# Four chained cross-attentions on one core: a fourth set of buffers and a new written-out order that puts alike TensorE steps side by side

## The chip, the core and the metric

The kernel runs on one core of a Trainium2 chip, in one launch. A core has five engines with instruction streams of their own: TensorE (PE in the profile, its weight loads PEld), VectorE (DVE), ScalarE (ACT), GpSimd (POOL) and SyncE (SP, which here only issues transfers). They meet through semaphores. All data are 32-bit floats. The metric is the device time of one launch in microseconds (us); lower is better. Matrix results go to PSUM, which the kernel treats as eight banks of 128 partitions by 512 floats.

## What is computed

128 batches of 64 query tokens (128 channels) attend to 64 context tokens (256 channels), four layers in a row. Layer 0 has 16 heads of 64 and a bias on a few key columns; layers 1 to 3 normalise x, have 16 query heads of 8 and 4 key/value heads. Cut to what matters:

```python
# layer 0
q = x @ Wq; k = ctx @ Wk; v = ctx @ Wv                 # 16 heads of 64
logits = einsum('bhqd,bhkd->bhqk', q, k) * 64 ** -0.5 + col_bias
out = einsum('bhqk,bhkd->bhqd', softmax(logits), v)
x = reshape(out) @ Wo + bo + x
# layers 1, 2, 3
xn = x * rsqrt(mean(x * x) + eps) * norm_w
q = xn @ wq; k = ctx @ wk; v = ctx @ wv                # 16 query heads of 8, 4 of k and v
scores = einsum('btgrd,bsgd->bgrts', q, k) / sqrt(8)
x = x + einsum('bgrts,bsgd->btgrd', softmax(scores), v) @ wo
```

## The kernel before

Four batches make a group (`G = 4`, 256 tokens); there are `NG = 32` groups. A group passes through named steps, written (kind, group, layer, unit). In the code they are branches of one loop per engine:

- TensorE, full 128x128 passes: `k` (L942, four steps), `v` (L954, six), `k3` (L961, keys of layers 1 to 3), `q0` (L969, four), `wo0` (L1027, the output projection of layer 0), and for each later layer `q` (L1032), `x2` (L1038, x transposed by full 128x128 passes, two into one bank, for the sum of squares) and `wo` (L1063).
- TensorE, with the array split into tiles: `s` of layer 0 (L980, 64x64, two steps), `s` of layers 1 to 3 (L991, 32x64, one step, four banks), `t` (L1009, the probabilities transposed, 64x128), `pv0` (L1019, 64x64, two steps) and `pv` (L1055, 128x32).
- VectorE: `add` (L1213), `max` (L1220, L1226), `sub` (L1230), `sum` (L1235), `rcp` (L1238), `wo0`, `wo` (L1257, residual added), `ssq`. GpSimd: `sub` of layer 0 (L888), `nrm` (L892, probabilities times 1/sum), `ms`. ScalarE: `exp` (L1136), `et` (L1141, the transposed probabilities copied from PSUM back to `E`), and the copies of `k`, `v`, `q0`, `pv0`, `x2`, `q`, `pv` out of PSUM. A group and layer have four units u of 128x512 probabilities each.

So the chain of one layer is q, s, max, sub, exp, sum, rcp, nrm, t, et, pv, wo, and then the next layer's q and x2. TensorE is kept at work meanwhile by the other groups in flight. A group's buffers (`xT`, `QT`, `E`, `st`, `nt`, `inv`) are chosen by `g % NS`, with `NS = 3`.

The order on each engine is written out: tables of numbers (`PE_TIME` and others) give every step a slot, group g is shifted by `g * PERIOD`, other tables (`PE_ENDS` and others) replace the numbers for the first and last groups, and `timed` sorts. The slots serve as sort keys; the engines wait on semaphores and on nothing else. In groups 30 and 31 (`SPLIT`) the later layers go in halves, and there the normalisation follows `pv` (L1049, L1248).

The PSUM banks are dealt out at build time. The loop walks the TensorE order; `free[i]` holds when the present contents of bank i are due to be emptied, by the table slots (`DUE`), and a step takes the bank or banks with the smallest `free`. Steps `s` of layers 1 to 3 take two neighbouring pairs:

```python
at = min(([i, i + 1, j, j + 1] for i in range(5) for j in range(i + 2, 7)),
         key=lambda four: max(free[i] for i in four))
```

At run time the step first waits until the step that emptied its bank has really ended (`emptied`), wherever its slot was.

## Time and profile before

| | |
|---|---|
| median of three runs | 1381.56 us (1379.52 to 1381.87) |
| span of the profiled execution | 1376.3 us |
| PE busy | 1362.7 us, 99% of the span |
| DVE, ACT, POOL busy | 1064.6, 1003.3, 734.9 us |
| PE in the chain that ended last | 95% |
| granted TensorE clock | full speed in every slice |

The median is 5.3 us above the profiled span; that is what lies around the span in a timed run. In a timeline row the first number is the start in us from the start of the span, the second the length, then engine, line, operation, what is written and read, the shape, and how many were merged into the row. A 32-bit matmul leaves two records; a transpose leaves one. The length of a PE row runs over the start of the next, since the array is pipelined, so the time that a block takes of PE is read from its start to the start of the next row. "[0.99 <-issue]" says that PE sat idle for that long before the row, and that no semaphore ended it.

### The profile page before, as it was taken

Reading aid. Unit: us, or ns where it says so; the run is one execution under the profiler, and the core shown is the slowest. Engines: PE = TensorE matmul, PEld = TensorE weight load, DVE = VectorE, ACT = ScalarE, POOL = GpSimd, SP = SyncE. Lnnn points to the kernel's source line nnn. Section 1 sums busy time; section 2 is a strip of 40 time slices with the busy share of each in tenths; the row PEclk is TensorE's granted clock in tenths of the full one; section 3 lists DMA queues with packets and bytes.
Section 4 is the critical chain, followed back from the end, with each engine's and each line's share of the span. In section 5 each row is a group of like instructions: output and inputs, shape, how many; then the busy total and the mean of one; then the engine's idle time right before and its main releaser. Section 6 shows DMA issues by size and latency. Waiting matters only on the chain.

```text
span 1376.3 us, 59054 instructions
## 1 busy us (share of the span) xinstructions
PE 1362.7 (99%) x25494; PEld 1055.6 (77%) x25494; DVE 1064.6 (77%) x2258; ACT 1003.3 (73%) x2207; POOL 734.9 (53%) x851
## 2 busy tenths in 40 slices
PE   9999999999999999999999999999999999999997
PEld 7777777777777777777787777777777777777875
DVE  4487777987778977778777788777798777778776
ACT  4667777767778677777677786777776777767886
POOL 5355456654456545466554565544665445655553
PEclk9999999999999999999999999999999999999999
DMA  5010010000000010100001001001011010010000
GB/s 151 18 30 22 15 34 16 26 27 23 26 23 22 27 27 23 28 18 26 26 24 26 23 22 27 27 24 28 17 27 27 23 27 25 19 36 22 7 23 14
DMA packets 46003, 37.02 MB, mean 27 GB/s; under 512 B 17072, under 2 KB 41520, under 8 KB 45744
## 3 DMA queue, kind: packets, MB, share of 16 engines
q1 hardware_dynamic: 44576, 32.89, 8.8%
q8 instruction: 201, 3.29, 1.0%
q14 instruction: 58, 0.48, 0.1%
q10 hardware_dynamic: 1168, 0.36, 0.1%
HBM read 16.42 MB, written 4.19 MB: 15 GB/s over the span
## 4 chain that ended last, share of the span: by engine, by line
PE 95%; ACT 2%; DVE 2%; issue 0%; POOL 0%; DMA 0%; SPq 0%; POOLq 0%
PE psum L954 18%; PE psum L942 16%; PE psum L1009 10%; PE psum L1027 8%; PE psum L969 8%; PE psum L991 7%; PE psum L1055 7%; PE psum L1019 5%; PE psum L980 5%; PE psum L1063 4%; PE psum L1032 3%; PE psum L961 2%; PE psum L1038 2%; ACT E L1141 1%; ACT E L1136 1%; DVE st L1226 1%
## 5 line engine op out<-in xcount | busy, mean ns | idle before, releaser
L892 POOL TENSOR_TENSOR E<-E,st 128x512 f32<-128x512 f32 x488 | 497.3, 1044 | 168.1 <-DVE st L1238 159.4
L1136 ACT ACTIVATE E<-E,inv 128x512 f32<-128x512 f32 x384 | 273.4, 722 | 135.8 <-DVE E L1230 134.3
L1226 DVE TENSOR_REDUCE st<-psum 128x8 f32<-128x512 f32 x372 | 240.4, 673 | 145.5 <-PE psum L991 145.1
L1235 DVE TENSOR_REDUCE st<-E 128x8 f32<-128x512 f32 x488 | 321.2, 665 | 35.3 <-ACT E L1129 28.2
L1141 ACT COPY E<-psum 128x512 f32<-128x512 f32 x512 | 275.1, 609 | 33.7 <-PE psum L1009 33.5
L954 PE MATMUL psum<-wv,cT 128*128 128x374 f32 (+1 forms) x768 | 273.3, 486 | 0.3 <-issue 0.3
L1230 DVE TENSOR_TENSOR E<-psum,st 128x512 f32<-128x512 f32 x372 | 248.3, 677 | 0.3
L904 POOL TENSOR_TENSOR nt<-nt,powers 128x2 f32<-128x2 f32 (+1 forms) x102 | 19.9, 196 | 420.0 <-DVE nt L1265 400.2
L942 PE MATMUL psum<-cT,wk 128*128 128x256 f32 x1024 | 240.5, 383 | 0.2 <-DMA cT<-in_ctx_t 0.2
L942 PEld LDWEIGHTS psum<-cT,wk 128*128 128x128 f32 x1024 | 191.5, 190 | 34.8 <-issue 1.5
L954 PEld LDWEIGHTS psum<-wv,cT 128*128 128x128 f32 x768 | 138.2, 189 | 73.5 <-ACT V L1097 8.5
L888 POOL TENSOR_TENSOR E<-E,st 128x512 f32<-128x512 f32 x140 | 142.6, 1044 | 35.8 <-DVE st L1220 13.1
L1009 PE MATMUL psum<-ident,E 64*128 64x64 f32 x4096 | 156.6, 226 | 3.5 <-issue 1.4
L1009 PEld LDWEIGHTS psum<-ident,E 64*128 64x128 f32 x4096 | 138.3, 139 | 20.0 <-issue 8.0
L969 PE MATMUL psum<-xq,wq 128*128 128x256 f32 x512 | 129.0, 385 | 0.0
L1027 PE MATMUL psum<-QT,wo 128*128 128x256 f32 (+1 forms) x544 | 119.1, 372 | 0.5 <-ACT QT L1163 0.5
L1055 PEld LDWEIGHTS psum<-E,VB 128*32 128x32 f32 x6144 | 90.9, 110 | 37.1 <-issue 14.7
L1097 ACT COPY V<-psum 128x374 f32<-128x374 f32 (+1 forms) x192 | 87.3, 456 | 42.9 <-PE psum L954 42.1
L1121 ACT ACTIVATE QT<-psum 128x512 f32<-128x512 f32 x128 | 75.9, 599 | 56.5 <-PE psum L969 48.2
L969 PEld LDWEIGHTS psum<-xq,wq 128*128 128x128 f32 x512 | 94.8, 190 | 23.1 <-issue 10.8
L991 PE MATMUL psum<-KB,QT 32*64 32x256 f32 x3072 | 109.2, 388 | 1.6 <-ACT QT L1160 1.0
L1027 PEld LDWEIGHTS psum<-QT,wo 128*128 128x128 f32 x544 | 96.2, 190 | 14.8 <-ACT QT L1163 0.6
(68 smaller groups left out, 1632.2 us busy)
## 6 DMA issues: line engine op xcount, KB each, us to landing
KB<-K SPq DMA_DIRECT2D x1536, 8.0 KB
cT<-in_ctx_t SPq DMA_DIRECT2D x32, 256.0 KB, 2.8
xq<-in_x_t SPq DMA_DIRECT2D x32, 128.0 KB, 2.1
out<-xT SPq DMA_DIRECT2D x30, 128.0 KB, 1.8
wk<-in_L_xattn_Wk SPq DMA_DIRECT2D x3, 256.0 KB, 5.8
wv<-in_L_xattn_Wv SPq DMA_DIRECT2D x2, 374.0 KB, 8.6
wq<-in_L_xattn_Wq SPq DMA_DIRECT2D x1, 512.0 KB, 7.7
wo<-in_L_xattn_Wo SPq DMA_DIRECT2D x1, 512.0 KB, 4.4
```

Of the source, the lines that this page charges most:

```text
L892: e.tensor_tensor(E3, E3, wide(stat[s][u][:, 16:24]), ALU.mult).then_inc(g_nrm.sem, 1)
L942: m = e.matmul(bank[:, T * jj:T * jj + T], wk0[:, k, 128 * j:128 * j + 128], cTg[:, k, :], start=(k == 0), stop=(k == 1))
L954: m = e.matmul(bank[:, 0:hi - lo], cTg[:, k, 128 * p:128 * p + 128], wv[:, k, lo:hi], start=(k == 0), stop=(k == 1))
L969: m = e.matmul(bank[:, T * jj:T * jj + T], wq0[:, 128 * j:128 * j + 128], xq[g % NX][:, :], start=True, stop=True)
L991: m = e.matmul(psum[64 * b2:64 * b2 + 64, at[r], 256 * p:256 * p + 256], QT[s][lo:lo + 32, 0, 64 * b:64 * b + 64], KB[l - 1][g % 2][lo:lo ...
L1009: m = e.transpose(psum[:, at[2 * n + i], c:c + 64], E[s][2 * p + r][rows, 128 * k:128 * k + 128], ident[rows, rows])
L1027: m = e.matmul(bank[:, tokens], wo0[:, j, :], QT[s][:, j, tokens], start=(j == 0), stop=(j == 7))
L1136: e.activation(E[s][u][:, :], E[s][u][:, :], ACT.Exp, scale=inv[s][:, u // 2:u // 2 + 1]).then_inc(a_exp.sem, 1)
L1141: e.copy(E[s][u][:, :], psum[:, i, :]).then_inc(a_et.sem, 1)
L1226: e.tensor_reduce(stat[s][u][:, 0:8].rearrange("p (r h) -> p r h", r=2), scores_of[g, l, u], AX, ALU.max).then_inc(d_max.sem, 1)
L1230: e.tensor_tensor(pairs(E[s][u][:, :]), scores_of[g, l, u], stat[s][u][:, 0:8].rearrange("p (r h a) -> p r h a", r=2, a=1).to_broadcast([1 ...
L1235: e.tensor_reduce(stat[s][u][:, 8:16], heads(E[s][u][:, :]), AX, ALU.add).then_inc(d_sum.sem, 1)
```

## The change

Three things differ; what is computed stays.

1. `NS` is 4 where it was 3, so four groups have buffers at a time.
2. All tables are new, with `PERIOD` 40.556641 where it was 42.042923. The tables for single groups now cover groups 0 to 7 and 28 to 31, and replace a group's table as a whole. Step `t` of groups 0 to 29 becomes two steps, one for two units each, with two banks instead of four and a wait of its own.
3. `DUE` is the slot plus a length by kind (`TAKES`), where it was the slot alone. The banks are dealt out anew from it. In the new tables for groups 28 to 31 a long row of steps has one and the same time: 16 of TensorE's steps stand at 1229.03 and 22 at 1270.13.

```diff
-NS = 3
+NS = 4
-PERIOD = 42.042923
+PERIOD = 40.556641
...
-    "t": {0: (-348.90236,), 1: (-317.45557,), 2: (-285.56016,), 3: (-253.49293,)},
+    "t": {0: (66.71164, 66.21564), 1: (98.14828, 97.59927), 2: (135.04492, 133.99991), 3: (176.09756, 175.10556)},
...
-        for kind, layers in {**table, **{k: {**table.get(k, {}), **v} for k, v in at_ends.get(g, {}).items()}}.items():
+        for kind, layers in at_ends.get(g, table).items():
...
-DUE = {tuple(st): at for at, *st in ACT_TIMED + DVE_TIMED}
+TAKES = {"k": 0.59, "v": 0.48, "k3": 0.36, "q0": 0.6, "pv0": 1.09, "x2": 0.39, "q": 0.37, "pv": 0.36, "se": 0.6, "et": 0.61,
+         "exp": 0.72, "add": 0.68, "max": 0.68, "sub": 0.68, "sum": 0.67, "rcp": 0.19, "wo0": 0.47, "ssq": 0.41, "lr": 0.33,
+         "lm": 0.29, "wo": 0.42}
+DUE = {(kind, g, l, u): at + (1.1 if kind == "v" and u % 3 == 2 else TAKES[kind])
+       for at, kind, g, l, u in ACT_TIMED + DVE_TIMED}
...
             if kind == "t":
-                return [[("et", g, l, 2 * p + i)] for p in halves(g, u) for i in range(2)]
+                return [[("et", g, l, 2 * u + i)] for i in range(2)]
...
-        p_t = signal("p_t", [("t", g, l, p) for _, g, l, u in of(PE_ORDER, "t") for p in halves(g, u)])
+        p_t = signal("p_t", of(PE_ORDER, "t"))
...
-                if kind != "t":
-                    emptied(w, [ev for evs in before[st] for ev in evs])
+                emptied(w, [ev for evs in before[st] for ev in evs])
...
-                    for n, p in enumerate(halves(g, u)):
-                        emptied(w, before[st][2 * n] + before[st][2 * n + 1])
-                        if late(g, l):
-                            w.wait_ge(a_exp, ("exp", g, l, 2 * p), ("exp", g, l, 2 * p + 1))
...
+                    if late(g, l):
+                        w.wait_ge(a_exp, ("exp", g, l, 2 * u), ("exp", g, l, 2 * u + 1))
...
-                    i = bank_of["t", g, l, part(g, u // 2)][u % 2 if g in SPLIT else u]
+                    i = bank_of["t", g, l, u // 2][u % 2]
```

Counted over the whole of TensorE's order, the new one goes from a full pass to a tiled step 159 times, where the old one did 235 times. Unbroken blocks of one tiled kind: `t` 104 for 131, `pv` 38 for 97, `pv0` 35 for 59, `s` of layers 1 to 3 98 for 102, `s` of layer 0 34 for 34. The number of matmuls is the same, 14891.

**Place 1, TensorE in the middle of the program.** L1055 or L1378 is `pv`, L1009 or L1332 is `t`, L980 or L1305 `s` of layer 0, KB and QT belong to `s`, wos to `wo`. Before, from one `pv` on:

```order
L1055 MATMUL psum<-E_0,VB 32x64 x8
L1055 MATMUL psum<-E_1,VB 32x64 x8
L1055 MATMUL psum<-E_2,VB 32x64 x8
L1055 MATMUL psum<-E_3,VB 32x64 x8
L1009 MATMUL psum<-ident,E_0 128x64 x8
L1009 MATMUL psum<-ident,E_1 128x64 x8
L1009 MATMUL psum<-ident,E_2 128x64 x8
L1009 MATMUL psum<-ident,E_3 128x64 x8
L1063 MATMUL psum<-QT,wos 128x256
L954 MATMUL psum<-wv,cT 128x372 x2
L1038 MATMUL psum<-ident,xT 128x128 x2
L1032 MATMUL psum<-xT,wqs 128x256
```

After, at the like place, from the second step of `s` of layer 0 on (four further rows of the third `pv` follow):

```order
L1305 MATMUL psum<-KT,QT 64x64 x64
L1332 MATMUL psum<-ident,E_2 128x64 x8
L1332 MATMUL psum<-ident,E_3 128x64 x8
L1332 MATMUL psum<-ident,E_0 128x64 x8
L1332 MATMUL psum<-ident,E_1 128x64 x8
L1378 MATMUL psum<-E_0,VB 32x64 x8
L1378 MATMUL psum<-E_1,VB 32x64 x8
L1378 MATMUL psum<-E_2,VB 32x64 x8
L1378 MATMUL psum<-E_3,VB 32x64 x8
L1378 MATMUL psum<-E_0,VB 32x64 x8
L1378 MATMUL psum<-E_1,VB 32x64 x8
L1378 MATMUL psum<-E_2,VB 32x64 x8
```

The `t`, `s` and `pv` steps of three groups now stand in one tiled stretch, where single ones stood between full passes. It begins with eight rows of `t` ahead of the ones shown.

**Place 2, TensorE at `s` of layer 3 in the middle of the program,** with the semaphores that a row waits for; a_et counts the copies `et`. Before (the `s` of group 16):

```order
L1063 MATMUL psum<-QT1,wos 128x256 [waits a_ev]
L954 MATMUL psum<-wv,cT0 128x374 x2
L1032 MATMUL psum<-xT1,wqs 128x256 [waits d_ev,d_add]
L1038 MATMUL psum<-ident,xT1 128x128 [waits a_et]
L1038 MATMUL psum<-ident,xT1 128x128
L954 MATMUL psum<-wv,cT0 128x374 x2
L991 MATMUL psum<-KB2_0,QT1 64x256 [waits l_kb2_0,a_et,a_ev]
L991 MATMUL psum<-KB2_0,QT1 64x256 x15
L954 MATMUL psum<-wv,cT0 128x372 [waits a_ev]
```

After (the `s` of group 16; E2 and `t` are those of layer 0 of group 18):

```order
L1332 MATMUL psum<-ident,E2_2 128x64 [waits g_nrm,a_ev]
L1332 MATMUL psum<-ident,E2_2 128x64 x7
L1332 MATMUL psum<-ident,E2_3 128x64 x8
L1332 MATMUL psum<-ident,E2_0 128x64 [waits g_nrm,a_ev]
L1332 MATMUL psum<-ident,E2_0 128x64 x7
L1332 MATMUL psum<-ident,E2_1 128x64 x8
L1316 MATMUL psum<-KB2_0,QT0 64x256 [waits d_ev,l_kb2_0,a_et,a_ev]
L1316 MATMUL psum<-KB2_0,QT0 64x256 x15
L1267 MATMUL psum<-cT1,wk0 128x256 x4
```

The `s` now stands directly behind a `t`, and one of its four banks is the one that this `t` filled first. That is so in 12 groups: 3, 8, 9, 11, 13, 14, 16, 18, 19, 21, 23 and 24.

**Place 3, TensorE at `s` of layer 1 of group 28,** with waits; d_sub counts VectorE's subtractions. Before:

```order
L969 MATMUL psum<-xq2,wq0 128x256 [waits a_ev]
L969 MATMUL psum<-xq2,wq0 128x256
L1063 MATMUL psum<-QT2,wos 128x256
L991 MATMUL psum<-KB0_0,QT1 64x256 [waits l_kb0_0,d_sub,a_ev]
L991 MATMUL psum<-KB0_0,QT1 64x256 x15
L954 MATMUL psum<-wv,cT2 128x374 [waits d_ev]
L954 MATMUL psum<-wv,cT2 128x374
L969 MATMUL psum<-xq2,wq0 128x256 [waits a_ev]
L969 MATMUL psum<-xq2,wq0 128x256
```

After:

```order
L1286 MATMUL psum<-cT0,wks 96x256 [waits d_sub]
L1286 MATMUL psum<-cT0,wks 96x256
L1316 MATMUL psum<-KB0_0,QT0 64x256 [waits a_ev,l_kb0_0,d_sub]
L1316 MATMUL psum<-KB0_0,QT0 64x256 x15
L1361 MATMUL psum<-ident,xT0 128x128 x2
L1294 MATMUL psum<-xq2,wq0 128x256 [waits l_xq2,d_sub]
L1294 MATMUL psum<-xq2,wq0 128x256 x3
L1294 MATMUL psum<-xq2,wq0 128x256 [waits a_ev]
L1294 MATMUL psum<-xq2,wq0 128x256
```

Behind the `s`, only an `x2` stands before a `q0` (L1294) that waits for d_sub: it has been dealt a bank that this very `s` filled, and waits for the third of its four subtractions. The same pair stands at `s` of layer 1 of group 29, with `q0` directly behind it. Behind `s` of layer 3 of group 27 stands a `v` of that kind, again for the third of four. Between groups 27 and 30 banks pass from step to step in other places too. With nothing between the two users of a bank stand: nine steps that wait for one copy of ScalarE (`pv0` of group 27 and of 28, `v` and `q` around them, `q0` of 29 and of 30, three `pv`), four that wait for one `wo` of VectorE, and, by `et`, twice each: the second `t` of layer 2 (with one `t` between), `s` of layer 0 behind four `t`, the second `t` of layer 1 into the banks of the first, for both of its copies, and the `pv` behind that. In the order before no step takes over a bank that the step directly ahead of it filled. Early in the new order there are two more: an `s` of layer 0 in group 9 (behind its own first step) and the `s` of layer 2 of group 8 (behind a `pv0`).

## Rows read from the trace of the kernel before

**Rows 1.** The page: busy us of each engine, share of the span, instructions.
```profile
PE 1362.7 (99%) x25494; PEld 1055.6 (77%) x25494; DVE 1064.6 (77%) x2258; ACT 1003.3 (73%) x2207; POOL 734.9 (53%) x851
```

**Rows 2.** Busy time by window: the last 44 us before the end.
```profile
1333.00:1377.00 44.00, 35.23 (x1016) 25.92 (x1004) 30.75 (x58) 29.79 (x72) 14.97 (x25) 1.00 0.06 17
```

**Rows 3.** Timeline of PE: the same step of two neighbouring groups (start, length, what).
```profile
560.15 3.62 PE L942 MATMUL psum<-cT,wk 128*128 128x256 f32 x16
...
601.99 1.24 PE L942 MATMUL psum<-cT,wk 128*128 128x256 f32 x5
```

**Rows 4.** Timeline of PE, 605 to 623: blocks and what follows each.
```profile
605.54 1.10 PE L1055 MATMUL psum<-E,VB 128*32 128x64 f32 x64
606.57 1.21 PE L1009 MATMUL psum<-ident,E 64*128 64x64 f32 x32
607.71 0.70 PE L1063 MATMUL psum<-QT,wos 128*128 128x256 f32 x2
608.25 1.41 PE L954 MATMUL psum<-wv,cT 128*128 128x372 f32 x4
...
609.71 0.60 PE L1032 MATMUL psum<-xT,wqs 128*128 128x256 f32 x2
610.24 1.16 PE L1019 MATMUL psum<-E,V 64*64 64x64 f32 x64
611.33 1.21 PE L1009 MATMUL psum<-ident,E 64*128 64x64 f32 x32
...
622.42 0.59 PE L1063 MATMUL psum<-QT,wos 128*128 128x256 f32 x2
622.85 0.38 PE L1038 MATMUL psum<-ident,xT 128*128 128x128 f32 x2
```

**Rows 5.** Timeline of PE: blocks of other lengths, each with the row behind it.
```profile
34.23 2.10 PE L1019 MATMUL psum<-E,V 64*64 64x64 f32 x128
36.25 1.99 PE L942 MATMUL psum<-cT,wk 128*128 128x256 f32 x8
...
1305.37 1.71 PE L1009 MATMUL psum<-ident,E 64*128 64x64 f32 x48
1307.01 1.52 PE L954 MATMUL psum<-wv,cT 128*128 128x374 f32 x4
...
1359.33 0.63 PE L1055 MATMUL psum<-E,VB 128*32 128x64 f32 x32
1359.89 1.07 PE L1063 MATMUL psum<-QT,wos 128*128 128x128 f32 x4
```

**Rows 6.** Waits of PE; the page's instruction queue; PE at 632; that queue in 631.50 to 631.75.
```profile
PE psum L1009 <- issue: 1.4, 2, 1.0
PE psum L1019 <- issue: 0.8, 3, 0.3
...
q8 instruction: 201, 3.29, 1.0%
...
632.05 0.90 PE L1009 MATMUL psum<-ident,E 64*128 64x64 f32 x22
633.94 0.53 PE L1009 MATMUL psum<-ident,E 64*128 64x64 f32 x10 [0.99 <-issue]
...
q8 instruction: 1, 0.02, 23.9%
```

**Rows 7.** Timeline of all engines: a transpose and the copy that empties its first bank.
```profile
589.77 1.21 PE L1009 MATMUL psum<-ident,E 64*128 64x64 f32 x32
...
590.53 0.59 ACT L1141 COPY E<-psum 128x512 f32<-128x512 f32 x1 [0.76 <-PE psum L1009]
```

**Rows 8.** Timeline: scores of a group, PE's next block, VectorE's third subtraction of them.
```profile
573.64 1.12 PE L991 MATMUL psum<-KB,QT 32*64 32x256 f32 x32
574.69 1.10 PE L1055 MATMUL psum<-E,VB 128*32 128x64 f32 x64
...
579.06 0.68 DVE L1230 TENSOR_TENSOR E<-psum,st 128x512 f32<-128x512 f32 x1
```

More of the change, by code:

```diff
@@ new lines @@
+    "sum": {0: (62.37469, 63.30765, 60.96066, 61.55667),
+            1: (90.35269, 92.57068, 93.16669, 93.76270),
+            2: (121.89328, 121.18826, 123.47629, 124.66830),
+            3: (164.62894, 163.43692, 161.14890, 165.92996)},
+    "rcp": {0: (63.08371, 65.05463, 62.97070, 62.26569),
+            1: (91.06171, 94.58072, 94.35870, 94.47171),
+            2: (126.56531, 131.50534, 127.59631, 130.80032),
+            3: (172.28400, 165.82095, 162.34091, 169.45795)},
+    "wo0": {0: (81.93265,)},
@@ L106 @@
-    "lt": {0: (-85.21396,)},
-    "st": {0: (-22.10277,)},
+    "cT": {0: (107.54190,)},
+    "kr": {1: (4.32867,), 2: (55.93527,), 3: (68.51465,)},
+    "lt": {0: (148.57855,)},
+    "st": {0: (241.79120,)},
 }
@@ new lines @@
+        "v": {0: (54.61811, 72.22778, 60.19144, 49.69811, 50.95478, 69.14044)},
+        "k3": {0: (53.75478,)},
+        "q0": {0: (48.83478, 58.46478, 64.43144, 59.32811)},
+        "s": {0: (68.09644, 67.11645), 1: (92.42812,), 2: (118.09644,), 3: (147.26279,)},
+        "t": {0: (79.52578, 77.81944),
+              1: (104.53478, 103.98578),
+              2: (138.26678, 137.71777),
+              3: (175.26511, 174.27312)},
+        "pv0": {0: (82.32411, 80.16978)},
+        "wo0": {0: (85.24678,)},
@@ new lines @@
+    4: {
+        "k": {0: (0.47821, 19.61655, 22.74222, 7.55588)},
+        "v": {0: (32.03989, 69.21321, 46.43622, 9.28255, -0.88245, 61.58421)},
+        "k3": {0: (2.63655,)},
+        "q0": {0: (41.94855, 43.46155, 50.67622, 45.46889)},
+        "s": {0: (54.74655, 53.76656), 1: (84.64522,), 2: (114.01822,), 3: (149.94354,)},
+        "t": {0: (65.64755, 65.09856), 1: (97.42822, 96.87921), 2: (134.45889, 133.41388), 3: (176.04355, 175.05154)},
+        "pv0": {0: (72.08655, 71.10056)},
+        "wo0": {0: (75.63321,)},
+        "x2": {1: (83.46889,), 2: (105.65622,), 3: (146.56488,)},
+        "q": {1: (83.03722,), 2: (111.46356,), 3: (145.91522,)},
+        "pv": {1: (99.84122,), 2: (138.70987,), 3: (180.72455,)},
+        "wo": {1: (104.36121,), 2: (144.62021,), 3: (186.57220,)},
+    },
@@ new lines @@
+        "et": {0: (77.19067, 77.19116, 77.19043, 77.19092),
+               1: (103.68823, 103.68799, 103.68774, 103.68750),
+               2: (165.42786, 164.94983, 161.93787, 163.03784),
+               3: (195.09155, 194.61353, 191.31348, 193.65747)},
+        "pv0": {0: (77.19238, 77.19214)},
+        "x2": {1: (94.87109,), 2: (133.86682,), 3: (173.55249,)},
+        "q": {1: (94.87085,), 2: (140.05188,), 3: (172.87354,)},
+        "pv": {1: (128.69482,), 2: (168.38989,), 3: (197.48145,)},
@@ new lines @@
+        "kr": {1: (58.15911,), 2: (80.25911,), 3: (91.30911,)},
+        "lt": {0: (158.56912,)},
+        "st": {0: (227.26912,)},
+    },
+    1: {
+        "cT": {0: (117.53247,)},
+        "kr": {1: (28.65247,), 2: (61.80247,), 3: (84.38247,)},
+        "lt": {0: (152.12247,)},
+        "st": {0: (187.67247,)},
+    },
+    2: {
+        "cT": {0: (111.08583,)},
+        "kr": {1: (32.29583,), 2: (54.87582,), 3: (77.93582,)},
+        "lt": {0: (145.67583,)},
+        "st": {0: (187.05981,)},
+    },
@@ new lines @@
+    3: {
+        "cT": {0: (104.63919,)},
+        "kr": {1: (25.36920,), 2: (48.42918,), 3: (71.48920,)},
+        "lt": {0: (106.07919,)},
+        "st": {0: (187.19385,)},
+    },
+    4: {
+        "cT": {0: (102.52621,)},
+        "kr": {1: (18.92255,), 2: (41.98254,), 3: (69.37622,)},
+        "lt": {0: (103.00623,)},
+        "st": {0: (187.72589,)},
+    },
+    5: {
+        "cT": {0: (101.13257,)},
+        "kr": {1: (12.47591,), 2: (39.86958,), 3: (67.98257,)},
+        "lt": {0: (101.61258,)},
+        "st": {0: (188.78925,)},
+    },
```

1128 lines of the change are left out of this document (690 added, 438 removed), and 88 rows, old and new, of tables (DVE_ENDS, PE_ENDS).

## The prediction, made before the changed kernel ran

> **What bounds the kernel now.** I read the page first. TensorE is busy for 1362.7 us, 99% of the span; the others have slack [rows 1]. TensorE idles mainly in the last 44 us, where 35.23 are busy and 8.8 are lost to hand-offs [rows 2]. In the middle there is next to none: the same step of two neighbouring groups starts at 560.15 and 601.99, 41.84 us apart [rows 3]. So the time is the length of TensorE's own list of steps, plus what it waits. A faster or slower neighbour changes nothing until TensorE waits for it.
>
> Next I read how long a block takes of TensorE, from its start to the start of the next row. A `wo` between full passes takes 0.43 us (622.42 to 622.85). A `wo` behind a `t` takes 0.54 (607.71 to 608.25), and a `q` of the same size ahead of a `pv0` takes 0.53 (609.71 to 610.24) [rows 4]. Going into tiled work and coming back costs 0.10 each. The tiled blocks have a fixed part too: `t` takes 1.64 us for 48 records [rows 5] and 1.14 for 32 [rows 4], so 0.50 for 16 and 0.14 for the block; `pv` 1.03 for 64 [rows 4] and 0.56 for 32 [rows 5], so 0.09 for the block; `pv0` 2.02 for 128 [rows 5] and 1.09 for 64 [rows 4], so 0.16. With such lengths laid end to end the old order gives 41.86 us for a group, against the 41.84 that I read. I trust them.
>
> **What the change removes.** The same matmuls run. Visits to tiled work fall from 235 to 159: 76 x 0.20 = 15.2 us. Blocks fall by 27 for `t` (x 0.14 = 3.8), by 59 for `pv` (x 0.09 = 5.3) and by 24 for `pv0` (x 0.16 = 3.8). The four fewer of `s` are left out. In sum 28 us go, all of them on the path, since TensorE is the path. The new order laid end to end gives 40.8 us for a group. The unknown is whether two `pv` of different groups join as cheaply as two halves of one; if not at all, 5.3 us less is saved, so 23 to 30.
>
> **What it adds: waits for banks.** A step can't start until its bank has been copied out. What that costs when nothing stands between the two users is read off a `t`: the block starts at 589.77, its first bank is full 0.64 us later (0.14 + 0.50), the copy starts at 590.53 and takes 0.59 [rows 7]. That is 0.12 to get there and 0.59 for the copy; I take as long again for the way back, 0.83 in all. No row shows such a pair, so its bounds are nothing, if the copy has some other way to be early, and 1.3, when the second copy is the one waited for.
>
> Middle: the `s` of layer 3 stands directly behind a `t` and needs its first bank in 12 groups (place 2). 12 x 0.83 = 10 us; bounds 0 and 16.
>
> Late groups (place 3). Three steps wait for the third subtraction of an `s` just ahead. In the trace an `s` starts at 573.64 and gives way at 574.69; VectorE's third subtraction of it starts at 579.06 and takes 0.68, so it ends 5.05 us after the `s` [rows 8]. VectorE has four maxima, three subtractions and a little more to do before that point, in the new order as well. With the `x2` in between (0.2) that is 4.8 and 5.0; the third, where one row of sums falls out, 4.5. Sum 14.3. Behind the waiting `q0` or `v` the whole of TensorE's queue stands still. Nine steps wait for one short copy: between the way alone (0.24) and a `t`'s 0.83, I take 0.6, as these copies are of half a bank: 5.4. Four wait for a `wo` of VectorE, also half a bank: 0.65 each, 2.6. Those by `et`, twice each: 0.83 less the 0.50 of the `t` between is 0.33, then 0.83, then both copies 1.33, then 0.83, together 6.6. The late groups lose 14.3 + 5.4 + 2.6 + 6.6 = 29 us. Bounds: 14 if only the three long ones bite, 35 if each short one costs a `t`'s.
>
> **What it adds: instruction supply.** TensorE idles in the middle almost only with "issue" named, 1.4 us in two places at `t` and 0.8 in three at `pv0`; the longest, 0.99, lies inside the `t` block that starts at 632.05 and resumes at 633.94. A transfer of the instruction queue begins 2.2 to 2.4 us before that end, in the window from 631.50. There are 201 such transfers of 3.29 MB, 16.4 KB each [rows 6]. TensorE has 25494 records, each with a weight load [rows 1], so one transfer brings about 254 instructions. Two steps `s` of layer 0 are 128 records or 256 instructions in 2.03 us: there TensorE runs out. Cut into lots of 254 along the block lengths, the old order has 6 to 8 lots that pass in under 2.4 us, the new one 36 to 38, for now `pv0` stands in pairs and `pv` in threes (384 instructions in under 3 us). Measured against the usual length of their kind, the blocks before are 3.8 us too long in total, 0.5 for each such lot. At 0.4 to 0.5 the new order would lose 14 to 20. I take 16, so 12 more than before; bounds 2 (a lot costs only what it falls short of 2.2 us) and 18.
>
> The Trainium skill ("Runtime: NRT & Kernel Launch", Instruction fetch mechanics) says that instructions stream in blocks of 16 KiB and that crossing into the next one is mostly hidden. The block size agrees with 16.4 KB; on the hiding, the 0.99 us speaks against it in dense stretches. By that rule this term would be nothing; it is the second rival.
>
> **What else.** The end: `t`, `pv` and `wo` of three and four groups stand together there, so the last results come out together and the chains have less beside them. Before, 8.8 us are lost in 44 [rows 2]. I take 6 more; bounds 0 and 12. Early groups have two bank pairs and a start with more to fill: 2, bounds 0 and 8. The fourth set of buffers costs nothing itself: it takes waits on older groups away, and TensorE had none of those.
>
> **The sum**, against the profiled execution: 1376.3 - 28 + 10 + 29 + 12 + 6 + 2 = 1407.3 us of span. The median of the runs lies 5.3 above the span: 1412.5 us. All low ends together give 1381.6 - 30 + 0 + 14 + 2 + 0 + 0 = 1368, all high ones 1381.6 - 23 + 16 + 35 + 18 + 12 + 8 = 1448.
>
> **The rivals.**
>
> *The banks come free in time.* The waits written into the order would then be met at once, because TensorE reaches those steps late or the copies run ahead. What is left is 1381.6 - 28 + 12 + 6 + 2 = 1373.5, faster than before. It decides at 8 us: if all bank waits together cost less, the change wins. For it speaks that in the old trace nearly every such wait is met early. Against it speaks that a copy can't start before the step that fills the bank ends, and here the next user stands directly behind.
>
> *Instructions come in time*, by the page's rule above. Then this term is -3.8 instead of +12: 1396.5. For it: only a few of the dense places before show idle time.
>
> *The chains are too tight in the middle.* In the old order 17.3 us of TensorE's work lie between `s` of layer 0 and its `t`, in the new one 10.2, with twelve passes of VectorE over 128x512 (at 0.6 to 0.68 us [rows 8]) in the chain. If `t` is late by 0.5 to 1 us in each group, 14 to 28 us come on top: about 1430. Against it: for layers 1 to 3 the distance grows or stays. Here also falls the case that joined blocks save nothing beyond the visits, 13 us, 1425.5.
>
> **How the numbers follow.** The forecast, 1412.5 with its own range of 1402 to 1424, has a chance of 0.60; banks in time 0.07; instructions in time 0.18; tight chains 0.12; something that none of these names 0.03. The range of 8 in 10 takes in the second rival and most of the third: 1392 to 1431. What a measurement can tell from no change is 0.2%, or 2.8 us. Only the first rival ends below 1378.8. Faster 0.07, same 0.03, slower 0.90.
>
> **What would show it.** In the profile after: distances of 40.8 us plus one or two waits between like steps of middle groups; in 12 of them 0.7 to 0.9 us of idle time ahead of the `s` of layer 3 with `et` named; three idle times of 4 to 5 us of TensorE with a subtraction of VectorE named, between 1180 and 1280, at `q0`, `v` and `q0`; some 15 us of idle time in tiled blocks put to "issue". A `q0` there without such a wait breaks the largest term. If the time is below 1380, it is the bank waits that I have wrong; if above 1431, the chains in the middle.

## The result: 8.4% slower, in the predicted direction and nearly four times the predicted amount

| | before | after |
|---|---|---|
| median | 1381.7 us | 1498.3 us |
| ratio, 95% interval | | 1.0843 [1.0826, 1.0861] |
| span of the profiled execution | 1376.3 us | 1494.2 us |
| PE busy | 1362.7 us, 99% | 1368.3 us, 92% |

I had forecast 1412.5, with 1392 to 1431 as the range. One of the four executions after took 1631.0 us at a granted clock of 0.84; the ratio leaves it out, and without it the median is 1497.4.

One number of the text ahead has to be set right here. Nearly every execution on record takes some 1.8 us more than its own span (the profiled one after: 1496.05 with a span of 1494.2). So of the 5.3 us between the median before and the profiled span only some 1.8 lie around the span; the rest is the difference between one execution and another. The forecast stays as it is, since its 31 us come on top of a median.

The page of the changed kernel: busy time and record counts, the granted clock in 40 slices, the instruction queue, and the chain of work that ended last (95% of it was TensorE before).

```profile
PE 1368.3 (92%) x25494; PEld 1074.8 (72%) x25494; DVE 1069.2 (72%) x2258; ACT 1010.3 (68%) x2207; POOL 734.6 (49%) x851
...
PEclk9999999999999999999999999999999999999998
...
q8 instruction: 201, 3.29, 0.9%
...
PE 62%; DVE 20%; ACT 12%; issue 6%; POOL 0%
```

The work is the same as in [rows 1]: same records, nearly the same busy time. What grew is the time in which TensorE stands still. Its waits (line waited at, who ended the wait: us in total, times, longest) name two kinds:

```profile
PE psum L1378 <- issue: 46.6, 37, 2.2
PE psum L1316 <- issue: 11.3, 17, 0.8
PE psum L1294 <- DVE E L1553: 9.3, 2, 4.7
PE psum L1332 <- issue: 5.1, 8, 1.0
...
PE psum L1279 <- DVE E L1553: 4.9, 2, 4.6
PE psum L1305 <- issue: 4.8, 10, 1.0
```

L1378 is `pv`, L1316 `s` of layers 1 to 3, L1332 `t`, L1305 `s` of layer 0, L1294 `q0`, L1279 `v`. Where [rows 6] had 1.4 and 0.8 us put to "issue", there are now 70.7. Twelve of the 17 waits at L1316 stand at the first record of a step; all the others put to "issue", 64 with 62.0 us, stand inside a block of one kind.

**Where the time went.** I took TensorE's order laid end to end, with the block lengths of the prediction, and cut it at the `wo0` of group 3 and of group 27. Before (L1027) and after (L1350):

```profile
156.08 3.72 PE L1027 MATMUL psum<-QT,wo 128*128 128x256 f32 x16
...
1164.27 3.72 PE L1027 MATMUL psum<-QT,wo 128*128 128x256 f32 x16
...
166.25 3.72 PE L1350 MATMUL psum<-QT,wo 128*128 128x256 f32 x16
...
1235.19 3.72 PE L1350 MATMUL psum<-QT,wo 128*128 128x256 f32 x16
```

| stretch | before: read, laid | after: read, laid | laid changes by | loss over laid changes by |
|---|---|---|---|---|
| to `wo0` of 3 | 156.1, 149.3 | 166.3, 153.7 | +4.4 | +5.8 |
| to `wo0` of 27 | 1008.2, 1003.7 | 1068.9, 979.6 | -24.1 | +84.8 |
| to the end | 212.0, 194.9 | 259.0, 186.1 | -8.8 | +55.8 |
| sum | 1376.3, 1347.9 | 1494.2, 1319.4 | -28.5 | +146.4 |

So the saving is there, 28.5 us, and 146.4 are lost on top: +117.9 of span. The laid lengths are an estimate from rows, good to some us.

**The middle.** TensorE's timeline in one group of it (start, length, line, what, records, idle time before):

```profile
716.93 2.20 PE L1332 MATMUL psum<-ident,E 64*128 64x64 f32 x64
719.23 2.14 PE L1305 MATMUL psum<-KT,QT 64*64 64x64 f32 x128
721.30 0.52 PE L1332 MATMUL psum<-ident,E 64*128 64x64 f32 x9
722.70 0.90 PE L1332 MATMUL psum<-ident,E 64*128 64x64 f32 x23 [0.89 <-issue]
723.53 1.66 PE L1378 MATMUL psum<-E,VB 128*32 128x64 f32 x104
727.19 1.44 PE L1378 MATMUL psum<-E,VB 128*32 128x64 f32 x88 [2.00 <-issue]
...
735.83 1.12 PE L1316 MATMUL psum<-KB,QT 32*64 32x256 f32 x32 [0.72 <-issue]
```

The stops at 722.70 and 727.19 lie in the middle of a step, where no semaphore is waited for. Between the two resumptions lie 23 + 104 = 127 records, 254 instructions with the weight loads: one lot, as the prediction calls what one transfer of the instruction queue brings. Transfers of that queue start at 720.25, 724.27 and 728.42; in the window from 724.25 to 724.50 it is

```profile
q8 instruction: 1, 0.02, 35.7%
```

TensorE resumes at 722.70 and 727.19, 2.5 and 2.9 us after the start of the transfer ahead. So it is throughout: all 59 stops inside a block up to 1235 us end 2.2 to 3.0 us after the start of a transfer. In 29 places a stop is followed by another 126 to 128 records behind, 3.3 to 4.5 us later, 3.8 on average. The second of such a pair is 1.35 us long on average, the other 35 stops 0.65: lots in a row are what costs.

Over the 25 groups from 100 to 1250 us the blocks of three `pv` are 52.9 us longer than the same block laid out (0.8 to 3.6 each), the two `s` of layer 0 and the `t` behind them 19.5.

The `s` of layer 3 behind a `t` waits 0.72 or 0.73 us in 12 groups, 8.7 in sum. They are just the 12 groups of place 2. In seven others between groups 5 and 22 the `s` stands behind a `t` too, but has been dealt other banks, and waits for nothing. So this wait is one for the bank, though the trace names "issue".

**The late groups.** The three long waits, where they were expected:

```profile
1293.85 4.24 PE L1294 MATMUL psum<-xq,wq 128*128 128x256 f32 x12 [4.60 <-DVE E L1553]
...
1331.23 2.86 PE L1279 MATMUL psum<-wv,cT 128*128 128x374 f32 x4 [4.57 <-DVE E L1553]
...
1354.04 3.78 PE L1294 MATMUL psum<-xq,wq 128*128 128x256 f32 x8 [4.66 <-DVE E L1553]
```

and busy time by window (last columns: granted clock, DMA share, GB/s):

```profile
1290.00:1376.00 86.00, 63.78 (x1166) 48.91 (x1166) 47.80 (x104) 46.36 (x99) 38.61 (x43) 0.92 0.05 15
...
1406.00:1494.00 88.00, 66.96 (x1874) 51.78 (x1871) 57.32 (x110) 56.70 (x129) 38.93 (x56) 0.92 0.04 11
```

22.2 and 21.0 us idle; the last 88 us before had 8.2. And the clock is not at full speed here, as it was in every slice before. From the `wo0` of group 27 on, TensorE is idle 48.2 us, where it was 8.8: 39.4 of the 55.8. Of the rest some 10 go to the clock, an estimate that the last part works out; some 6 stay open.

### The profile page after: what moved, and what is told of

The parts are those of the page before. It is cut to its first block, busy times and chain, and to the rows that moved or that the text cites. A ratio compares the mean times of both kernels' runs of the same rounds, so it can differ in the third digit from the quotient of the medians.

```text
span 1494.2 us, 58934 instructions
## 1 busy us (share of the span) xinstructions
PE 1368.3 (92%) x25494; PEld 1074.8 (72%) x25494; DVE 1069.2 (72%) x2258; ACT 1010.3 (68%) x2207; POOL 734.6 (49%) x851
## 4 chain that ended last, share of the span: by engine, by line
PE 62%; DVE 20%; ACT 12%; issue 6%; POOL 0%
PE psum L1267 11%; PE psum L1279 10%; PE psum L1332 7%; PE psum L1378 7%; DVE st L1549 6%; DVE st L1558 6%; PE psum L1316 6%; DVE E L1553 5%; PE psum L1305 4%; ACT E L1459 4%; PE psum L1342 4%; PE psum L1294 3%; PE psum L1350 3%; PE psum L1386 3%; ACT E L1464 2%
## 5 line engine op out<-in xcount | busy, mean ns | idle before, releaser
L1558 DVE TENSOR_REDUCE st<-E 128x8 f32<-128x512 f32 x488 | 310.5, 671 | 90.5 <-ACT E L1452 55.7
L1549 DVE TENSOR_REDUCE st<-psum 128x8 f32<-128x512 f32 x372 | 240.3, 682 | 117.9 <-PE psum L1316 117.8
L1459 ACT ACTIVATE E<-E,inv 128x512 f32<-128x512 f32 x384 | 260.7, 719 | 88.0 <-DVE E L1553 83.9
L1464 ACT COPY E<-psum 128x512 f32<-128x512 f32 x512 | 262.3, 617 | 37.9 <-PE psum L1332 36.8
L1279 PE MATMUL psum<-wv,cT 128*128 128x374 f32 (+1 forms) x768 | 278.1, 486 | 6.6 <-DVE E L1553 4.9
L1267 PE MATMUL psum<-cT,wk 128*128 128x256 f32 x1024 | 249.5, 387 | 1.2 <-issue 1.0
L1553 DVE TENSOR_TENSOR E<-psum,st 128x512 f32<-128x512 f32 x372 | 241.1, 678 | 1.5
L1279 PEld LDWEIGHTS psum<-wv,cT 128*128 128x128 f32 x768 | 143.5, 192 | 79.1 <-issue 10.3
L1332 PE MATMUL psum<-ident,E 64*128 64x64 f32 x4096 | 154.6, 227 | 13.0 <-issue 5.1
L1332 PEld LDWEIGHTS psum<-ident,E 64*128 64x128 f32 x4096 | 138.3, 139 | 38.3 <-issue 23.6
L1378 PE MATMUL psum<-E,VB 128*32 128x64 f32 x6144 | 106.4, 222 | 50.9 <-issue 46.6
L1536 DVE TENSOR_TENSOR E<-psum,bias 128x512 f32<-128x512 f32 x128 | 82.2, 683 | 88.7 <-PE psum L1305 88.7
L1420 ACT COPY V<-psum 128x276 f32<-128x276 f32 (+1 forms) x192 | 84.4, 440 | 85.0 <-PE psum L1279 85.0
L1378 PEld LDWEIGHTS psum<-E,VB 128*32 128x32 f32 x6144 | 93.4, 111 | 61.2 <-issue 54.3
L1294 PE MATMUL psum<-xq,wq 128*128 128x256 f32 x512 | 127.0, 389 | 10.7 <-DVE E L1553 9.3
L1316 PE MATMUL psum<-KB,QT 32*64 32x256 f32 x3072 | 114.0, 392 | 15.7 <-issue 11.3
L1294 PEld LDWEIGHTS psum<-xq,wq 128*128 128x128 f32 x512 | 96.2, 194 | 31.7 <-DVE E L1553 10.0
L1350 PE MATMUL psum<-QT,wo 128*128 128x256 f32 (+1 forms) x544 | 117.1, 369 | 0.6 <-ACT QT L1469 0.4
```

Source lines behind the costliest of these rows:

```text
L1267: m = e.matmul(bank[:, T * jj:T * jj + T], wk0[:, k, 128 * j:128 * j + 128], cTg[:, k, :], start=(k == 0), stop=(k == 1))
L1279: m = e.matmul(bank[:, 0:hi - lo], cTg[:, k, 128 * p:128 * p + 128], wv[:, k, lo:hi], start=(k == 0), stop=(k == 1))
L1294: m = e.matmul(bank[:, T * jj:T * jj + T], wq0[:, 128 * j:128 * j + 128], xq[g % NX][:, :], start=True, stop=True)
L1316: m = e.matmul(psum[64 * b2:64 * b2 + 64, at[r], 256 * p:256 * p + 256], QT[s][lo:lo + 32, 0, 64 * b:64 * b + 64], KB[l - 1][g % 2][lo:lo ...
L1332: m = e.transpose(psum[:, at[i], c:c + 64], E[s][2 * u + r][rows, 128 * k:128 * k + 128], ident[rows, rows])
L1378: m = e.matmul(bank[32 * r:32 * r + 32, 64 * b:64 * b + 64], VBg[:, b, c:c + 32], E[s][b][:, n:n + 64], start=(gp == 0), stop=(gp == 1))
```

## The experiments

My theory after the result: (1) in the middle, instructions don't come fast enough, and lots that follow each other cost far more than the single ones of the old trace; (2) in the late groups, the banks. The rivals: steps of different groups don't join on the array, the chains of the groups are too tight, the fourth set of buffers costs. All ratios are to the kernel before, run on the same chip at the same time (1380.1 to 1381.8 us).

**The supply by itself.** The kernel before, with this ahead of its first step:

```diff
+            for n in (64, 96, 112, 128):
+                for i in range(320):
+                    r = i % 4
+                    e.matmul(psum[32 * r:32 * r + 32, 7, 0:n], blank[:, 0:32], blank[:, 0:n], start=True, stop=True)
+                for _ in range(32):
+                    e.matmul(psum[:, 6, 0:128], blank, blank, start=True, stop=True)
```

> The kernel before with dense work ahead of everything else: four stretches of 320 tiled matmuls (128x32 tiles, four column groups in turn, blank data) of 64, 96, 112 and 128 columns, each followed by 32 full passes of 128 columns. They write to a bank that is overwritten later, so the output stays. A stretch is five lots of 254 instructions. By the pace of a pv (32 matmuls of 64 columns in 0.94 us) the stretches would take 9.4, 14.1, 16.5 and 18.8 us. Theory A (a lot can't be fetched before the one ahead of it has begun, and lots that follow each other take about 4.1 us each, as read from the changed kernel): 64 columns about 2.2 us of idle time per lot, 96 columns 1.3, 112 columns 0.8, 128 columns 0.4; put to issue. Theory B (my prediction's: a lot costs 0.4 to 0.5 us when it passes in under 2.4 us, otherwise nothing): 0.5 per lot at 64 columns, nothing at 96 and above. Theory C (nothing to do with instructions): no idle time at all. Whole time by A about 1460 us, by B about 1450, by C about 1447.

Measured 1482.96 us in one run. Timeline of PE, the stretches of 64, 96, 112 and 128 columns:

```profile
12.38 3.38 PE L925 MATMUL psum<-E 128*32 128x64 f32 x128 [4.37 <-issue]
17.75 2.77 PE L925 MATMUL psum<-E 128*32 128x64 f32 x128 [1.99 <-issue]
21.48 2.30 PE L925 MATMUL psum<-E 128*32 128x64 f32 x128 [0.96 <-issue]
...
33.36 5.81 PE L925 MATMUL psum<-E 128*32 128x96 f32 x271
39.80 2.84 PE L925 MATMUL psum<-E 128*32 128x96 f32 x128 [0.63 <-issue]
43.53 2.85 PE L925 MATMUL psum<-E 128*32 128x96 f32 x128 [0.88 <-issue]
47.53 2.55 PE L925 MATMUL psum<-E 128*32 128x96 f32 x113 [1.16 <-issue]
...
66.08 3.27 PE L925 MATMUL psum<-E 128*32 128x112 f32 x128 [0.46 <-issue]
69.81 3.27 PE L925 MATMUL psum<-E 128*32 128x112 f32 x128 [0.46 <-issue]
73.26 1.41 PE L925 MATMUL psum<-E 128*32 128x112 f32 x49 [0.18 <-issue]
...
81.94 17.67 PE L925 MATMUL psum<-E 128*32 128x128 f32 x640
```

From stop to stop there are always 128 records. The distance between two stops is 3.73 us in most cases, with 64, 96 and 112 columns alike (17.75 to 21.48, 39.80 to 43.53, 66.08 to 69.81). It is no fixed floor: the others are 5.37 (12.38 to 17.75), 4.00 (43.53 to 47.53) and 3.45 (69.81 to 73.26). The 5.37 falls into a time when the data come in (all queues together moved 311 GB/s from 13 to 18 us, 5 at most from 26 us on); whether that is the reason was not tested. With 128 columns a lot takes 17.6 / 5 = 3.5 by itself, and no stop is seen. The first lots of a stretch pass: 271 records of 96 columns run without a stop, two lot boundaries among them, though a lot takes 2.84 there; the third boundary costs 0.63, the next 0.88 and 1.16.

So the threshold in my prediction was wrong, and the price with it. A lot is short when it passes in under 3.5 to 4 us, not under 2.4, and once a few short ones have followed each other, each costs the difference. Theory A had the kind of it right, and the pace nearly (4.1); it had named 0.4 per lot at 128 columns, where there is none. B and C fall by the rows. The whole time decides nothing, as 1483 lies above all three (1460, 1450, 1447): they had left some 8 us for the full passes between the stretches, an estimate, and 64 records of these take 7.41, four times. The Trainium skill ("Runtime: NRT & Kernel Launch", Instruction fetch mechanics) calls the crossing from one block of instructions to the next mostly hidden. That agrees with the stretch of 128 columns and not with the other three.

**Does the stop follow the instructions?** The changed kernel with half a lot more at the start:

```diff
+            for i in range(32):
+                e.matmul(psum[32 * (i % 4):32 * (i % 4) + 32, 7, 0:64], blank[:, 0:32], blank[:, 0:64], start=True, stop=True)
```

> The changed kernel, with 32 tiled matmuls (64 records, about 128 instructions, half a lot) more at the very start, where TensorE waits for its first data anyway. Theory A (the idle time inside a block stands where a lot of about 254 instructions begins): in the block of three pv in which TensorE stands still behind record 104 of 192 (at 725.2 us of the changed kernel) it now stands still about 64 records earlier, behind record 40, and the one behind record 9 of 32 of the t ahead moves into s of layer 0. The whole time moves by less than 10 us either way. Rival (it stands where data or the array decide): it stays behind record 104.

Measured 1509.7 us in one run. The same group as above (L1307 is `s` of layer 0, L1334 `t`, L1380 `pv`):

```profile
723.49 1.42 PE L1307 MATMUL psum<-KT,QT 64*64 64x64 f32 x74
725.07 1.04 PE L1307 MATMUL psum<-KT,QT 64*64 64x64 f32 x54 [0.15 <-issue]
...
727.17 0.77 PE L1380 MATMUL psum<-E,VB 128*32 128x64 f32 x40
728.96 1.99 PE L1380 MATMUL psum<-E,VB 128*32 128x64 f32 x128 [1.02 <-issue]
732.29 0.54 PE L1380 MATMUL psum<-E,VB 128*32 128x64 f32 x24 [1.34 <-issue]
```

Behind record 40, as expected to the record; the one in `t` has moved into `s` (record 74, 9 - 64 + 128 = 73 expected), and a second boundary now falls into the same block of `pv` (40 + 128 + 24 = 192). The data and the array are as before. The stop belongs to the place in the stream of instructions. The whole time moved by 11 us, a little more than the 10 that I had allowed; 1 us of it is the added work itself (the `v` that starts at 18.00 starts at 19.03 here), for TensorE was not idle where it stands.

**Fewer instructions in the same order.**

```diff
...
-                        for gp in range(2):
+                        for gp in range(1 if g < NG - 4 else 2):
...
```

> The changed kernel, with the second half of the matmuls of every pv left out in groups 0 to 27 (the values of one of the two halves of heads are missing from the output). The order is unchanged, the three pv still stand together. 84 steps get 0.47 us shorter, 39 us. Theory A (instruction supply): the three together are then 192 instructions instead of 384, the 53 us of idle time in them vanish too: 1498 - 39 - 53 = about 1406, down to 1395 if the idle time at the t behind shrinks too. Rival (the join of different groups costs about 0.7 us whatever its length): 1459.

Measured 1430.8 (1.0366 [1.0350, 1.0382]): 67 us less, 28 more than the left out work. That lies between the two, 1406 and 1459; 25 us of what theory A has did not go. The waits at `pv`:

```profile
PE psum L1378 <- ACT E L1464: 12.0, 19, 0.7
PE psum L1378 <- issue: 10.0, 16, 1.1
```

The stops named issue went from 46.6 to 10.0, as theory A has it. But 12.0 us now go to the copies of `t` (L1464), where it was 2.3: the block ahead is shorter and covers them no more. The steps are joined as before, so a fixed cost of the join, the rival's 0.7 us, is not what the stops were.

**Passes between the pv.** In groups up to 29 a `k` or `v` from behind goes between two `pv` in a row:

```diff
...
+            for pv in run:
+                mixed += [pv] + behind[len(mixed) // 2:len(mixed) // 2 + 1]
...
```

> The changed kernel, with a k or v step of TensorE from behind put between pv steps that stand in a row (groups up to 29), and its copy on ScalarE moved with it; nothing else. The changed kernel is at 1498. Theory A (instruction supply): the 53 us by which the blocks of three pv are too long in the middle go nearly all; two more visits to tiled work per group (0.20 each) and two more blocks (0.09 each) cost 14 us in 25 groups: about 1460, and the idle time named issue inside pv falls from 47 us to under 5. Rival (the three-fold block is slow since the steps of different groups don't join: what is lost is lost per step): apart they would each still be too long, and the time stays at 1498 or above.

Measured 1469.9 (1.0651 [1.0634, 1.0669]): 28 us less than the change as it is. "Issue" at `pv` is 8.9 us where it was 46.6. Here L1404 is `pv`, L1342 `s` of layers 1 to 3:

```profile
PE psum L1342 <- issue: 12.2, 17, 1.2
PE psum L1404 <- issue: 8.9, 13, 1.1
```

The order laid end to end is 15.7 us longer, since every parting costs a visit to tiled work and a block. By the profiled spans (1494.2 and 1470.8) 39 us of loss went and 16 of the saving. I had expected 1460, with under 5 us of issue at `pv`; the parted blocks still hold an occasional stop. The rival, 1498 or above, falls.

**The banks.**

```diff
...
+        elif kind == "s":
...
+                    DUE[e, g, l, i] = now + LAG[e] + 0.68 * (i % 2 if l == 0 or g in SPLIT else i)
...
```

> The changed kernel, with the due times of the banks in the stretch of slots 1140 to 1290 taken from TensorE's list laid end to end (with 0.85 to 1.5 us for a copy and 4.0 and more for the subtractions, never earlier than the one ahead in its queue), instead of the slots of the copies. Orders are unchanged; only banks are dealt otherwise. Theory A (the waits in the late groups come from banks dealt by slots that all read 1229.03 and 1270.13): the waits of 4.60, 4.57 and 4.66 us and most short ones go, 21 us of the 29; the granted clock of 0.91 to 0.93 behind them goes to 1.00 and gives back about 5: 1498 - 26 = 1472. Rival (the waits stand for the chains of the late groups, which end when they end): the time stays within 5 us of 1498, idle time comes back with other names.

Measured 1477.2 (1.0711 [1.0684, 1.0738]), 21 us less, where I had expected 26. No order was touched. A window of this kernel, and a row of its timeline:

```profile
1290.00:1333.00 43.00, 40.74 (x760) 32.28 (x754) 32.08 (x69) 31.31 (x68) 22.57 (x26) 1.00 0.08 23
...
1339.61 1.85 PE L1330 MATMUL psum<-xq,wq 128*128 128x256 f32 x4 [3.51 <-DVE E L1589]
```

Two of the three long waits are gone, and so is the fall of the clock between 1290 and 1333 (0.93 in the changed kernel); one wait of 3.51 is left, and behind it four records of `q0` take 1.85 us, not 1.03.

**Both together.**

> The changed kernel with both edits that helped alone: passes between the pv steps (alone 1469.9, 28 us less) and due times of the late stretch from TensorE's list (alone 1477.2, 21 us less). If the two losses are separate things, as my theory has it (instruction supply in the middle, banks in the late groups), their gains add: 1498.3 - 28.4 - 21.1 = 1449. Rival (both are the same lack of slack seen twice): the gains overlap, and it stays above 1458.

Measured 1447.5 (1.0473 [1.0458, 1.0488]). By the medians the gains add within 2 us; by the ratios, each to the kernel before of its own time, the two alone give 45 us and both together 51, which is at the edge of the noise. They do not overlap, so instruction supply and late banks are two separate losses. With both edits the kernel is still 66 us slower than before: TensorE is idle for 77.6 us of the profiled 1453.8, 37.0 of them named issue, and the granted clock is 0.95 from 1235 us on. No run takes these apart.

**All passes spread.** With the new due times, four full passes per group go between tiled steps (two `pv` also change places where their copies come in the other order):

```diff
...
+MOVES = (("v", 1, 3, "s", 0, 0, 1), ("k", 1, 1, "t", -1, 1, 1), ("v", 0, 5, "pv", -1, 1, 0), ("v", 0, 1, "s", -2, 3, 0))
...
```

> The changed kernel with two edits. First, the due times of the banks in the late stretch as in the run before (1477). Second, in groups 5 to 28 four full passes go to new places of TensorE's order and their copies with them: a v between t and s of layer 0, a k between s of layer 0 and the t behind, a v between the first and the second pv, and a v between t and s of layer 3. Theory A (what is lost in the middle is instruction supply and the bank wait at s of layer 3): of 53 us at pv, 20 at s of layer 0 and the t behind, and 9 at s of layer 3, some 70 go, while four more visits to tiled work and the blocks that they cut cost 1.0 per group, 23 us: 1477 - 70 + 23 = 1430; idle time named issue falls from 68 to under 15 us. Rival (the chains of the groups are the limit, as in my third rival): TensorE waits for named engines instead, the time stays above 1455.

Measured 1526.9 (1.1059 [1.1041, 1.1077]): 97 us slower than expected, and 50 slower than with the due times alone. The waits (L1369 `s` of layers 1 to 3, L1385 `t`, L1439 `wo`):

```profile
PE psum L1369 <- DVE E L1606: 20.7, 19, 1.1
PE psum L1385 <- POOL E L1271: 17.1, 40, 1.3
...
PE psum L1439 <- ACT QT L1539: 7.4, 29, 0.7
```

The rival has it: named engines, and a time above 1455. Theory A is right in one part only: "issue" fell to 15.8 us in all. But now every group waits for named engines: `t` for the normalisation (it stands 1.25 us earlier), `s` of layer 2 for a bank of `s` of layer 3 (passes between them were taken away), `wo` for copies that stand behind a moved one. In this order the chains had no slack for such moves, so my third rival is real once passes are moved. I did not find an order that has both the joins and the slow lots; whether there is one stays open.

**The other term: buffers.**

> The kernel before, with a fourth set of buffers for the groups and nothing else. My prediction: costs and gives nothing, 1380 to 1383 us. Rival (some waits on the buffers of three groups before bind in the old order): up to 5 us faster. Another (the larger footprint costs): slower.

Measured 1381.25, 0.9998 [0.9989, 1.0007]. Nothing, as predicted.

**The clock.** Ahead of each of the three steps that wait long:

```diff
...
+                if st in KEEP:
+                    emptied(w, [ev for evs in before[KEEP[st]] for ev in evs])
+                    for _ in range(10):
+                        e.matmul(psum[:, bank_of[KEEP[st]][0], 0:T], ident[:, :], wk0[:, 0, 0:T], start=True, stop=True)
...
```

> The changed kernel, with ten full passes of 256 columns that nobody needs (4.3 us) ahead of each of the three steps that wait 4.6 us for a subtraction (q0 and v of group 29, q0 of group 30), into a bank that is free then. Theory A (the granted clock falls because TensorE stood still, and the 12, 4 and 8 records behind take 1.4 to 1.9 us longer each for that reason): they go back to 2.6, 1.3 and 1.7 us, and the time falls by 3 to 6 us, though TensorE has more to do: 1493. Rival (the clock falls in these stretches for another reason, or the records are long since their operands come late): no change, 1498, or slower by up to 1.

Measured 1497.7 (1.0836 [1.0814, 1.0858]), no change that the noise of some 4 us would let one see. Yet the rows did what theory A says:

```profile
1239.39 3.72 PE L1356 MATMUL psum<-QT,wo 128*128 128x256 f32 x16
...
1298.36 2.86 PE L1300 MATMUL psum<-xq,wq 128*128 128x256 f32 x12 [0.28 <-DVE E L1559]
...
1335.47 1.52 PE L1285 MATMUL psum<-wv,cT 128*128 128x374 f32 x4
...
1356.81 1.99 PE L1300 MATMUL psum<-xq,wq 128*128 128x256 f32 x8 [0.28 <-DVE E L1559]
```

12, 4 and 8 records took 2.86, 1.52 and 1.99 us instead of 4.24, 2.86 and 3.78, 4.5 us less: they were slow because TensorE had stood still. But the time did not fall. From the `wo0` of group 27 to the end it is 1498.6 - 1239.4 = 259.2 us, against 259.0. The trace shows where much of it went: the lower clock comes back further on, behind the short waits for copies. The `pv` behind the first place, in the changed kernel and here:

```profile
1312.65 1.10 PE L1378 MATMUL psum<-E,VB 128*32 128x64 f32 x64 [0.68 <-ACT E L1464]
...
1315.79 1.62 PE L1384 MATMUL psum<-E,VB 128*32 128x64 f32 x64 [0.68 <-ACT E L1470]
```

The granted clock is 1.00 from 1312 to 1318 there, and 0.86 from 1312 to 1324 here; at the next such place it is 0.83 from 1370 to 1380. So this run does not show what the lower clock costs as a whole, only that it moves on when the long waits alone are filled. Also, this `wo0` starts 4.2 us later than in the changed kernel though all the program ahead of it is the same: the stops in the middle differ that much between executions.

**Turned on the old order.** If only fixed parts counted, a join inside one visit would be a gain:

```diff
...
+        if pe["pv0", g, 0, 1] < pe[t] < pe[late]:
+            pe[late] = pe[t] - 0.01
+            act[late] = min(act["et", g - 2, 3, u] for u in range(4)) - 0.01
...
```

> The kernel before, in which pv0, t, pv0 of groups 5 to 27 becomes pv0, pv0, t, and the copies on ScalarE follow. A join inside one visit: the instructions of the visit stay the same, so no lot becomes denser, and one block start of 0.16 us goes per group. Theory (what a join saves is its fixed part, as in my sum, as long as it brings no lot under the pace of the instruction supply): 23 x 0.16 = 3.7 us less, 1378 beside 1381.8. Rival (the t and its four copies come 0.9 us later, and pv of layer 3 waits for them): the gain is used up, within 1 us of before or slower.

Measured 1389.7 (1.0054 [1.0041, 1.0066]): 8.4 us slower, not 3.7 faster. The rival's words allow it ("or slower"), its mechanism does not: the idle time that came is not named after copies. Timeline:

```profile
869.79 1.73 PE L1031 MATMUL psum<-E,V 64*64 64x64 f32 x99
873.00 0.69 PE L1031 MATMUL psum<-E,V 64*64 64x64 f32 x29 [1.48 <-issue]
```

"Issue" comes to 12.4 us in all, against 2.5 before. A `t` of 32 records takes as long as a `pv0` of 64, so the `t` between two `pv0` was what kept that lot at 2.8 us; without it the lot passes in 2.0. I had said that no lot becomes denser since the visit stays the same. The lot, not the visit, is what counts. To part this from mere places of lots, both orders with half a lot more at the start:

> The kernel before with 32 tiled matmuls (half a lot of instructions) more at the very start, so that every lot begins at another place of the same order. Theory A (the old order has nearly no idle time since it keeps every lot slow enough, wherever the lots begin): 1380 to 1384 us, idle time named issue in the middle under 6 us. Theory B (it has little because its lots happen to begin in good places, and what made the pairing of pv0 8 us slower was that places moved): 1386 us or more.

> The kernel before with pv0, pv0, t in place of pv0, t, pv0 (alone 1389.7, of before 1.0054) and the same 32 matmuls more at the start. Theory A (two pv0 in a row put 127 records into 2.0 us where pv0, t, pv0 has them in 2.8; that costs wherever a lot begins near there, in about as many groups as before): 1386 to 1393 us, idle time named issue in the middle 8 to 15 us. Theory B (chance of the places): anywhere between 1377 and 1395, with no tie to the pairing; together with the run beside it at 1386 or more.

Measured 1387.9 (1.0053 [1.0036, 1.0070]) and 1396.1 (1.0116 [1.0101, 1.0131]). The pairing costs 8 us in either position (1389.7 - 1381.3, 1396.1 - 1387.9), so it costs by itself, as theory A of the second has it. The 1396.1 and its 16.7 us of "issue" lie just outside that theory's ranges all the same (1386 to 1393, 8 to 15), and outside those of theory B. For the old order alone is slower by 7 us in the shifted position, which was theory B of the first. The 32 matmuls take 2 us of this themselves (`s` of layer 0 starts at 19.93 us, 17.89 before); the rest is the shift: "issue" comes to 10.0 us there, for 2.5, two of the stops in `pv` blocks of the last 25 us (2.9). So the 2.5 us are partly owed to where the lots begin.

## Why the prediction was right in sign and wrong in size

1. **The saving, 28 us: right.** The laid orders differ by 28.5. That joined steps of different groups save their fixed part holds too, at least where no stop falls in: a `pv` block of 192 records without a stop takes 2.82 us in the run with new due times (1305.86 to 1308.68), three of 1.03 would take 3.09. That is 0.13 for each of the two joins, where I had 0.09.
2. **Bank waits of `s` of layer 3, +10: right,** 8.7 read, at 0.72 or 0.73 each for 0.83. The trace puts them to "issue", not to the copies that I had named as the sign.
3. **Late bank waits, +29: right in mechanism, step and length, a little large.** 4.60, 4.57 and 4.66 for 4.8, 5.0 and 4.5, at the `q0`, `v` and `q0` that I had named; they end at 1293.9 to 1354.0, not between 1180 and 1280, since the middle is so much longer. Idle time between 1290 and 1376 is 22.2; dealing the banks anew gave back 21 us in all, with one wait of 3.51 left.
4. **Instruction supply, +12: the step that failed.** In the middle the loss over the laid order grew by 84.8 us. Less the 8.7 of point 2, some 76 are left for this term, of which the rows of `pv` and of `s` of layer 0 with its `t` show 72. The step was "the new one 36 to 38 [lots in under 2.4 us] ... at 0.4 to 0.5". Both factors were too small. TensorE stops 64 times inside a block, not 37 times; that 37 of these stops are at `pv` is chance. The limit of 2.4 us had left out every lot that passes in 2.4 to some 3.8 us. And a stop costs 1.0 us on average (62.0 / 64), 1.26 at `pv` (46.6 / 37), up to 2.2. I had read the price off single short lots, between slow ones, in an order in which it was small also because of where its lots begin. My upper bound of 18 came from the same single lots, so the range was no protection. The old trace held no two lots under 2.4 us in a row; I should have said that its rows give no upper bound. A whole transfer for each lot (2.2 to 2.4 us, 37 lots, 81 to 89 us) would have been one that holds here.
5. **The end, +6: too small.** In the last 88 us 21.0 are idle, 8.2 before: 12.8.
6. **The clock, not in the sum at all.** At 0.92 in two windows of 86 and 88 us, TensorE ran 16% of them, 28 us, at 1.2 GHz and not at 2.4. Where it was busy that lost half, an estimate of 10 us. I had the three idle times and did not ask what comes behind them. The run that kept TensorE at work in the three long waits got 4.5 us back there and nothing in the whole, since the lower clock came back further on; what it costs as a whole stays an estimate. The Trainium skill ("TensorE: Matmul & The Clock Gate", Part 1) says that the clock is gated down to half when the array has been idle; these rows agree.
7. **Start, +2:** 5.8.

The rivals: banks in time and instructions in time are refuted. The tight chains were not what made the change slow, though my last sentence would have blamed them for any time above 1431; with the passes moved they are what keeps the cure that I tried from working. The sign was right for reasons that held: the bank waits came as forecast (8.7 us, and 21 given back by dealing the late banks anew) and already outweigh the 28.5 saved. No rival came near 1498: it falls to the 0.03 that none of them names.

## What to carry to other kernels

A gathered order saves switches of TensorE and makes its instructions denser; count the time that each 128 matmul records take in the new order, wherever they lie, and distrust every place where several in a row take under some 3.8 us. A small loss of a kind that the old trace shows only singly is no price for a row of them: ask for an upper bound that does not come from those rows. Read "issue" idle time by place: inside a step it was the instruction stream here, at the first record of a step it could be a bank wait.

## What the runs showed of the hardware

- 128 records of tiled matmuls (256 instructions with the weight loads) followed each other, where one stop came behind another, 3.3 to 4.5 us apart in the middle of the program (29 pairs, 3.8 on average) and 3.45 to 5.37 in the probe, mostly 3.73. The first one or two lots of a stretch passed faster, and lots of 3.5 us showed no stop.
- All 59 stops of the changed kernel inside a block up to 1235 us end 2.2 to 3.0 us after the start of a transfer of the instruction queue.
- Half a lot of instructions more at the start moved a tuned program of 1381 us by 7 us and the gathered one by 11; the added work itself is 2 and 1 of these. (The 11 is from one run, of a kernel whose middle differs by 4 us between executions.)
- Behind an idle time of 4.6 us matmuls took up to twice as long (4 records 2.86 us, not 1.52), and not where full passes that nobody needs had filled it.
